# A one-layer adaLN, attention and sparse FFN kernel: the last group's expert marks and spread pattern at full array size

## The chip, the cores and the metric

The kernel runs on one core of one Trainium2 chip. A core has five engines that run side by side and wait for each other through semaphores: TensorE (PE; its matmuls, and apart from them the loads of the stationary operand, PEld), VectorE (DVE), ScalarE (ACT), GpSimd (POOL) and SyncE (SP), which starts most DMAs. The metric is the device time of one execution in microseconds; the kernel before takes 114.97 us, the median of three runs (114.91 to 114.98).

## What is computed

The input is 2048 tokens of 128 features. The reference, cut to what matters:

```python
x = L0_attn_y_all
h = layernorm(x) * (1 + ca) + sa
x = x + ga * attention(h, Wq, bq, Wk, bk, Wv, bv, Wo, bo)       # causal, one head of 128
h = layernorm(x) * (1 + cb) + sb
x = x + gb * ffn(h)

def ffn(x):                                                     # 16 experts, blocks of 32 of 512 channels
    prob = softmax(x @ w_router + b_router)
    _, idx = top_k(prob, 4)
    mask = (idx[:, :, None] == arange(16)).any(axis=1)          # 4 of 16 experts for a token
    h = relu(einsum('nd,ebd->neb', x, w1b) + b1b)
    y = einsum('neb,ebd,ne->nd', h, w2b, mask)
    return y + b2
```

All scale and shift vectors come from `silu(c) @ wmod`. What counts here is the mask: a token's hidden channels of the 12 experts that it did not choose must be zero.

## The kernel before

The tokens are 16 tiles of 128, in 4 groups of 4 tiles (512 tokens). A tile `[P, 512]` holds one group with features or channels on the 128 partitions. Values that need more precision than one pass gives are kept as a high and a low part of type float32r, and a product is three matmuls: high by high, low by high, high by low (`three`, lines 928, 929 and 932). Each engine has its own program, and the order of its steps is written out by hand in a table (`TENSOR_PLAN`, `SCALAR_PLAN`, `VECTOR_PLAN`, `GPSIMD_PLAN`): a letter names a step, a number its tile. Every step begins with the semaphores that it waits for.

On TensorE the last group's end of the plan reads `d8 h11 d9 d10 m3 y0 h12 v12 h13 v13 y1 d11 h14 v14 h15 v15 d12 d13 y2 d14 d15 t0 y3 t1`. Here `h` is an up-projection tile (three matmuls of 512 columns), `d` a down-projection tile (three matmuls), `y` turns a finished group back to rows of tokens (fp32 transposes, line 1168), `t` computes the last two token tiles directly in rows (line 1139), `m` turns the choice of experts and `v` is explained below.

The choice. `choose` on DVE finds a token's four largest router logits and marks them. For groups 0 to 2 it writes each expert's mark eight times over (`chosen`, 128 columns in bf16), `turn_choice` on TensorE transposes four blocks of 128 by 128 into `norm_bank` (line 1108), and ScalarE copies them out as `keep`, by which DVE multiplies the hidden channels (line 841). The four hidden tiles of a group share one `keep`, since the channels are dealt so that partition q of each tile belongs to expert q // 8.

For the last group (`shut_by_tensor`) TensorE does the masking. `choose` writes one mark for each expert, 1 where it was not chosen (`unchosen`, `[P, 4, 16]` bf16, line 826). `turn_choice` transposes them: `unchosen[:, i]` with its 16 columns is the stationary operand and the identity moves, four times (line 1103). ScalarE copies the 16 by 512 result to `shut` (line 637). Then `shut_channels` (`v12` to `v15`, line 1133) adds `spread.T @ shut` to the hidden tile in PSUM; `spread` is 16 by 128 and has -1e30 where a channel belongs to an expert, so each channel of a shut expert falls far below zero and relu makes it zero. ScalarE reads the tile twice (lines 652 and 653, high part and the last 256 columns), and DVE subtracts for the low part (line 850), which the down-projection's third matmul reads.

`spread` is built by GpSimd at the start (`prepare(4)`, lines 502 to 507, fourth step of its plan): memset, two selects that keep a band, one cast. In the plan it stands ahead of `j0`, the first half group's 1/sigma (lines 439 and 440), for which DVE waits before it normalises the first tokens (line 706). A `step` on GpSimd adds to `pool_step` and waits for it; `ahead` adds without waiting.

Of the kernel before, what the change touches and what calls it, by code (L numbers as in the profile page):

```python
# [5 lines left out]
ALU = mybir.AluOpType  # L6
# [4 lines left out]
BF16 = mybir.dt.bfloat16  # L11
# [11 lines left out]
P = 128  # L23
GT = 4
GW = GT * P
EPS = 1e-5
FAR = -1e30
FURTHEST = 3e38
# [42 lines left out]
def adaln_attention_sparse_ffn(nc, x_in, wq_in, bq_in, wk_in, bk_in, wv_in, bv_in, wo_in, bo_in,  # L71
# [3 lines left out]
    NBLK = wr_in.shape[1]  # L75
# [4 lines left out]
    NH = HID // P  # L80
# [52 lines left out]
    with ExitStack() as ctx:  # L133
        def sb(name, shape, dt=F32):
            return ctx.enter_context(nc.sbuf_tensor(name, shape, dt))

        def sem(name):
            return ctx.enter_context(nc.semaphore(name))
# [4 lines left out]
        ctx_bank, norm_bank, proj_bank = bank[5], bank[6], bank[7]  # L143
# [64 lines left out]
        rden = sb("rden", [P, NT])  # L208

        shut_by_tensor = (NG - 1,)  # L210
        shut, spread = sb("shut", [NBLK, GW], BF16), sb("spread", [NBLK, P], BF16)
        spread_full = sb("spread_full", [NBLK, P])
        unchosen = sb("unchosen", [P, GT, NBLK], BF16)


        swung_sums = sb("swung_sums", [P, GT, 2, NBLK])
# [3 lines left out]
        marked = sb("marked", [P, GT, KEYS])  # L220
# [13 lines left out]
        ident_made, copies_made, causal_made, future_made, unseen_made, warm_made, filler_made, base_made, ones_made, keys_made, spread_made = (  # L234
            sem(n) for n in ("ident_made", "copies_made", "causal_made", "future_made", "unseen_made", "warm_made", "filler_made", "base_made", "ones_made", "keys_made", "spread_made"))
# [176 lines left out]
        def _(pool):  # L412
# [6 lines left out]
            def step(ins):  # L419
                ahead(ins)  # L420
                pool.wait_ge(pool_step, steps[0])
# [38 lines left out]
            def prepare(i):  # L460
                if i == 0:
                    pool.memset(pow_half[:], -0.5)
                    step(pool.memset(ident[:], 0.0))
                    pool.affine_select(out=ident[:], in_=ident[:], compare_op=ALU.not_equal, fill=1.0, base=0,
                                       pattern=[[-1, P]], channel_multiplier=1).then_inc(ident_made, 1)
                elif i == 6:
                    pool.wait_ge(mod_out, 1)
                    gates()
                elif i == 1:
                    step(pool.memset(causal_full[:], 0.0))  # L470
                    step(pool.affine_select(out=causal_full[:], in_=causal_full[:], compare_op=ALU.is_ge, fill=FAR, base=0,
                                            pattern=[[-1, P]], channel_multiplier=1))
                    pool.tensor_copy(causal[:], causal_full[:]).then_inc(causal_made, 1)
                elif i == 7:
                    step(pool.memset(future[:, GW - P:], 0.0))
                    pool.affine_select(out=future[:, GW - P:], in_=future[:, GW - P:], compare_op=ALU.is_ge, fill=FAR, base=0,
                                       pattern=[[-1, P]], channel_multiplier=1).then_inc(future_made, 1)
                elif i == 8:
                    step(pool.memset(unseen[:], 0.0))
                    pool.affine_select(out=unseen[:], in_=unseen[:], compare_op=ALU.is_ge, fill=FAR, base=0,  # L480
                                       pattern=[[1, P]], channel_multiplier=-1).then_inc(unseen_made, 1)
                elif i == 9:
                    pool.wait_ge(w1_hi_s, 1)
                    pool.tensor_tensor(w1t_lo[:], w1_full[:], w1t_hi[:].bitcast(F32), ALU.subtract).then_inc(w1_lo_s, 1)
                elif i == 11:
                    pool.wait_ge(wr_full_s, 1)
                    pool.wait_ge(wr_in_s, 32)
                    step(pool.tensor_tensor(wr_full[0:1, :], wr_full[0:1, :], br_row[:], ALU.add))
                    step(pool.tensor_copy(wr_halves[:, 0, :], wr_full[:]))
                    pool.tensor_tensor(wr_halves[:, 1, :], wr_full[:], wr_halves[:, 0, :].bitcast(F32),  # L490
                                       ALU.subtract).then_inc(wr_s, 1)
                elif i == 10:
                    pool.wait_ge(w2_hi_s, 1)
                    pool.tensor_tensor(w2t_lo[:], w2_full[:], w2t_hi[:].bitcast(F32), ALU.subtract).then_inc(w2_lo_s, 1)
                elif i == 12:
                    pool.wait_ge(gbb2_row_s, 1)
                    pool.wait_ge(*emptied(f"o{NG - 1}", 1))
                    for i in range(2):
                        last = pool.tensor_tensor(x_due[:, i, :], x[:, NT - 2 + i, :], gbb2_row[:], ALU.add)
                    last.then_inc(x_due_s, 1)  # L500
                elif i == 4:
                    step(pool.memset(spread_full[:], FAR))
                    step(pool.affine_select(out=spread_full[:], in_=spread_full[:], compare_op=ALU.is_ge, fill=0.0, base=0,
                                            pattern=[[1, P]], channel_multiplier=-PER))
                    step(pool.affine_select(out=spread_full[:], in_=spread_full[:], compare_op=ALU.is_ge, fill=0.0,
                                            base=PER - 1, pattern=[[-1, P]], channel_multiplier=PER))
                    pool.tensor_copy(spread[:], spread_full[:]).then_inc(spread_made, 1)
# [16 lines left out]
        def _(act):  # L524
# [109 lines left out]
            def keep_copy(g):  # L634
                act.wait_ge(chosen_turned, g + 1)
                if g in shut_by_tensor:
                    nc.scalar.copy(shut[:], norm_bank[0:NBLK, 0:GW // 2].bitcast(BF16)).then_inc(keep_s, 1)
                else:
                    keeps, chose = grp(keep, g), norm_bank[:, 0:GW // 2].bitcast(BF16)
                    if g in SWUNG:  # L640
                        keeps = keeps.rearrange("c (i b t) -> c b i t", i=GT, b=GT)
                        chose = chose.rearrange("c (b i t) -> c b i t", i=GT, b=GT)
                    nc.scalar.copy(keeps, chose).then_inc(keep_s, 1)
# [26 lines left out]
        def _(dve):  # L670
# [146 lines left out]
            def choose(g):  # L817
                dve.wait_ge(keys_s, g + 1)
                for i in range(GT):
                    last = nc.vector.max(top8[:, i, :], keys[:, i, :])  # L820
                step(last)
                for i in range(GT):
                    last = nc.vector.match_replace(marked[:, i, :], top8[:, i, :], keys[:, i, :], FURTHEST)
                step(last)
                if g in shut_by_tensor:
                    nc.vector.tensor_scalar(unchosen[:], marked[:, :, 0:NBLK], FURTHEST, None, ALU.is_lt).then_inc(chosen_s, 1)
                    return
                if g >= 1:
                    dve.wait_ge(chosen_turned, g)
                each = marked[:, :, 0:NBLK].rearrange("p i (e o) -> p i e o", o=1).broadcast_to([P, GT, NBLK, PER])  # L830
                nc.vector.tensor_tensor(chosen[:], each, highest(g).rearrange("p (i e o) -> p i e o", e=1, o=1).broadcast_to(
                    [P, GT, NBLK, PER]), ALU.is_gt).then_inc(chosen_s, 1)
# [89 lines left out]
        def _(pe):  # L922
# [176 lines left out]
            def turn_choice(g):  # L1099
                pe.wait_ge(chosen_s, g + 1)  # L1100
                if g in shut_by_tensor:
                    for i in range(GT):
                        last = nc.tensor.transpose(norm_bank[0:NBLK, i * P // 2:(i + 1) * P // 2].bitcast(BF16),
                                                   unchosen[:, i], ident_b[:])
                    last.then_inc(chosen_turned, 1)
                    return
                for i in range(GT):
                    last = nc.tensor.transpose(norm_bank[:, i * P // 2:(i + 1) * P // 2].bitcast(BF16),
                                               chosen[:, i].rearrange("p e k -> p (e k)"), ident_b[:])
                last.then_inc(chosen_turned, 1)  # L1110
# [17 lines left out]

            def shut_channels(n):
                pe.wait_ge(keep_s, n // NH + 1)  # L1130
                if n == NH * shut_by_tensor[0]:
                    pe.wait_ge(spread_made, 1)
                mm(turned_bank(f"h{n}")[:], spread[:], shut[:], start=False, stop=True).then_inc(turn_mm, 1)  # L1133

            def down_rows(i):
# [139 lines left out]
```

## Time and profile before

| what | value |
|---|---|
| time, median of 3 runs | 114.97 us (114.91 to 114.98) |
| span of the profiled execution | 113.2 us, 2012 instructions |
| PE matmuls busy | 109.0 us (96%), x585 |
| PE weight loads busy | 87.6 us (77%) |
| DVE busy | 87.3 us (77%) |
| ACT busy | 74.3 us (66%) |
| POOL busy | 88.1 us (78%) |
| granted TensorE clock, mean | 1.000, that is 2.4 GHz |

The span runs from the first to the last instruction of the one execution that was profiled; its own device time isn't given apart, and the median of the runs stands for it, 1.77 us above the span. The page says that matmuls are pipelined and their ends modelled: two matmuls whose busy times overlap run one behind the other, and the distance of their starts tells what the first cost. A matmul row has a partner on PEld, the load of its stationary operand, which can run under the matmul ahead of it; "idle before" on a PEld row is time in which no load ran. In a row, `128*16` behind the names is rows by columns of the stationary operand, `16*128` likewise.

### The profile page before, as it was taken

Reading aid. Unit: us, or ns where it says so; the run is one execution under the profiler, and the core shown is the slowest. Engines: PE = TensorE matmul, PEld = TensorE weight load, DVE = VectorE, ACT = ScalarE, POOL = GpSimd, SP = SyncE. Lnnn points to the kernel's source line nnn. Section 1 sums busy time; section 2 is a strip of 40 time slices with the busy share of each in tenths; the row PEclk is TensorE's granted clock in tenths of the full one; section 3 lists DMA queues with packets and bytes.
Section 4 is the critical chain, followed back from the end, with each engine's and each line's share of the span. In section 5 each row is a group of like instructions: output and inputs, shape, how many; then the busy total and the mean of one; then the engine's idle time right before and its main releaser. Section 6 shows DMA issues by size and latency. Waiting matters only on the chain.

```text
span 113.2 us, 2012 instructions
## 1 busy us (share of the span) xinstructions
PE 109.0 (96%) x585; PEld 87.6 (77%) x585; DVE 87.3 (77%) x322; ACT 74.3 (66%) x163; POOL 88.1 (78%) x118
## 2 busy tenths in 40 slices
PE   5999999999999999999999999999999999999991
PEld 2588769878888888888877878788898888856590
DVE  5999989999999999978897399708974846854251
ACT  1346398497973499677498995988815578435610
POOL 6869868998999199989899999999992898916000
PEclk9999999999999999999999999999999999999999
DMA  2894000000000000000000000000000000003314
GB/s 60 266 336 130 3 0 6 0 3 0 0 3 0 6 0 0 0 0 3 0 0 6 0 0 0 0 0 0 0 6 3 0 3 0 0 0 93 98 56 129
DMA packets 5879, 3.42 MB, mean 30 GB/s; under 512 B 743, under 2 KB 5483, under 8 KB 5868
## 3 DMA queue, kind: packets, MB, share of 16 engines
q1 hardware_dynamic: 5292, 3.03, 9.0%
q10 hardware_dynamic: 576, 0.26, 0.9%
q8 instruction: 5, 0.08, 0.3%
q14 instruction: 6, 0.05, 0.1%
HBM read 2.24 MB, written 1.05 MB: 29 GB/s over the span
## 4 chain that ended last, share of the span: by engine, by line
PE 81%; DVE 13%; issue 2%; POOL 2%
PE bank L928 14%; PE bank L929 13%; PE bank L932 13%; PE bank L1040 7%; PE bank L988 7%; PE bank L1027 6%; PE bank L1028 6%; PE bank L1072 3%; PE bank L962 2%; PE bank L1168 2%; PE bank L1139 2%; DVE nmax L743 1%; DVE st L686 1%; POOL rstd L440 1%; PE bank L1133 1%
## 5 line engine op out<-in xcount | busy, mean ns | idle before, releaser
L512 POOL TENSOR_TENSOR p_lo<-p_full,p_hi 128x512 fp32r<-128x512 f32 (+2 forms) x36 | 42.5, 1206 | 4.6 <-ACT p_full L626 4.5
L619 ACT ACTIVATE p_hi<-bank 128x512 fp32r<-128x512 f32 (+2 forms) x36 | 20.6, 571 | 6.6 <-PE bank L932 2.9
L626 ACT ACTIVATE p_full<-bank 128x512 f32<-128x512 f32 (+2 forms) x36 | 20.5, 568 | 0.6 <-POOL p_lo L512 0.6
L518 POOL TENSOR_TENSOR hid_lo<-hid_full,hid_hi 128x512 fp32r<-128x512 f32 x12 | 15.4, 1294 | 5.3 <-ACT hid_hi L655 5.3
L748 DVE TENSOR_REDUCE cmax<-bank 128x1 f32<-128x512 f32 x24 | 16.1, 685 | 2.0 <-PE bank L988 1.7
L1027 PE MATMUL bank<-g_hi,zt_hi 128*128 128x512 f32 (+3 forms) x40 | 15.2, 381 | 0.0
L1040 PE MATMUL bank<-g_lo,zt_hi 128*128 128x512 f32 (+3 forms) x40 | 14.6, 373 | 0.2 <-DVE g_lo L768 0.2
L1028 PE MATMUL bank<-g_hi,zt_lo 128*128 128x512 f32 (+3 forms) x40 | 14.6, 364 | 0.0
L928 PE MATMUL bank<-p_hi,z_hi 128*128 128x512 f32 (+2 forms) x36 | 14.0, 389 | 0.0
L988 PE MATMUL bank<-zt_hi,g_hi 128*128 128x512 f32 (+3 forms) x40 | 13.8, 386 | 0.0
L929 PE MATMUL bank<-p_hi,z_lo 128*128 128x512 f32 (+2 forms) x36 | 13.5, 374 | 0.0
L932 PE MATMUL bank<-p_lo,z_hi 128*128 128x512 f32 (+2 forms) x36 | 13.4, 373 | 0.0
L841 DVE SCALAR_TENSOR_TENSOR hid_full<-bank,keep 128x512 f32<-128x512 f32 x12 | 8.1, 686 | 5.6 <-POOL hid_lo L518 2.7
L590 ACT ACTIVATE xn<-x,mean_rstd,rstd 128x127 f32<-128x127 f32 x24 | 9.9, 485 | 0.3 <-POOL mean_rstd L433 0.3
L655 ACT CAST hid_hi<-hid_full 128x512 fp32r<-128x512 f32 x12 | 7.4, 622 | 3.0 <-DVE hid_full L841 2.4
L1040 PEld LDWEIGHTS bank<-g_lo,zt_hi 128*128 128x128 f32 x40 | 7.5, 188 | 1.8 <-issue 0.7
L988 PEld LDWEIGHTS bank<-zt_hi,g_hi 128*128 128x128 f32 x40 | 7.5, 189 | 1.4 <-ACT g_hi L605 0.2
L1027 PEld LDWEIGHTS bank<-g_hi,zt_hi 128*128 128x128 f32 x40 | 7.5, 189 | 1.1
L1028 PEld LDWEIGHTS bank<-g_hi,zt_lo 128*128 128x128 f32 x40 | 7.6, 189 | 0.9
L430 POOL TENSOR_TENSOR rstd<-rstd,pow_half 128x4 f32<-128x4 f32 x7 | 7.3, 1038 | 0.6
L928 PEld LDWEIGHTS bank<-p_hi,z_hi 128*128 128x128 f32 x36 | 6.8, 188 | 1.2
L932 PEld LDWEIGHTS bank<-p_lo,z_hi 128*128 128x128 f32 x36 | 6.8, 188 | 1.2
(212 smaller groups left out, 256.1 us busy)
## 6 DMA issues: line engine op xcount, KB each, us to landing
x<-in_L_attn_y_all_dram SPq DMA_DIRECT2D x3, 256.0 KB, 3.5
out_dram<-res SPq DMA_DIRECT2D x3, 256.0 KB, 2.3
w<-in_L_ffn_w_dram SPq DMA_DIRECT2D x2, 256.0 KB, 4.2
x<-in_L_attn_y_all_dram SPq DMA_DIRECT2D x2, 128.0 KB, 2.9
wmod<-in_L_wmod_dram SPq DMA_DIRECT2D x1, 256.0 KB, 3.7
wmod<-in_L_wmod_dram ACTq DMA_DIRECT2D x1, 128.0 KB, 3.2
out_dram<-res SPq DMA_DIRECT2D x1, 128.0 KB, 1.9
wk<-in_L_attn_Wk_dram SPq DMA_DIRECT2D x1, 64.0 KB, 2.9
```

The source lines that it names most:

```text
L512: pool.tensor_tensor(p_lo[:, s, w:], p_full[:, n % 2, w:], p_hi[:, s, w:].bitcast(F32), ALU.subtract).then_inc(p_lo_pool, 1)
L518: pool.tensor_tensor(hid_lo[:, m, :], hid_full[:, n % 2, :], hid_hi[:, m, :].bitcast(F32), ALU.subtract).then_inc(hid_lo_pool, 1)
L619: nc.scalar.activation(p_hi[:, s, w:], src, ACT.Exp).then_inc(p_hi_s, 1)
L626: nc.scalar.activation(p_full[:, n % 2, w:], src, ACT.Exp).then_inc(p_full_s, 1)
L748: nc.vector.tensor_reduce(cmax[:, n, c:c + 1], src, AX.X, ALU.max, negate=True).then_inc(turn_out, 1)
L928: mm(dst, w_hi, m_hi, start=start, stop=False)
L929: mm(dst, w_lo, m_hi, start=False, stop=False)
L932: return mm(dst, w_hi, m_lo, start=False, stop=stop)
L988: last = mm(dst[:, 0:w], tile(g_hi, g * GT + r), zt_hi[:, c * GW:c * GW + w], start=True, stop=not masked)
L1027: mm(dst[:, w:], tile(zt_hi, j), high, start=True, stop=False)
L1028: mm(dst[:, w:], tile(zt_lo, j), high, start=False, stop=False)
L1040: last = mm(dst[:, w:], tile(zt_hi, j), g_lo[:, g * GW + w:(g + 1) * GW], start=False, stop=not diag)
```

## The change

Three tensors of the last group's choice get the full array size. `unchosen` has 128 columns for each token tile, of which GpSimd clears the last 112 at the start; `spread` and `spread_full` have 128 rows, in which the selects leave rows 16 to 127 at zero; `shut` has 128 rows, which the transposes fill with the turned marks and zeros. DVE still writes 16 marks for each token tile. The wait for `spread_made` stands ahead of the transposes instead of ahead of the first shut matmul. The plans are unchanged.

```diff
@@ -208,9 +208,9 @@
         rden = sb("rden", [P, NT])
 
         shut_by_tensor = (NG - 1,)
-        shut, spread = sb("shut", [NBLK, GW], BF16), sb("spread", [NBLK, P], BF16)
-        spread_full = sb("spread_full", [NBLK, P])
-        unchosen = sb("unchosen", [P, GT, NBLK], BF16)
+        shut, spread = sb("shut", [P, GW], BF16), sb("spread", [P, P], BF16)
+        spread_full = sb("spread_full", [P, P])
+        unchosen = sb("unchosen", [P, GT, P], BF16)
 
 
         swung_sums = sb("swung_sums", [P, GT, 2, NBLK])
@@ -499,6 +499,7 @@
                         last = pool.tensor_tensor(x_due[:, i, :], x[:, NT - 2 + i, :], gbb2_row[:], ALU.add)
                     last.then_inc(x_due_s, 1)
                 elif i == 4:
+                    ahead(pool.memset(unchosen[:, :, NBLK:], 0.0))
                     step(pool.memset(spread_full[:], FAR))
                     step(pool.affine_select(out=spread_full[:], in_=spread_full[:], compare_op=ALU.is_ge, fill=0.0, base=0,
                                             pattern=[[1, P]], channel_multiplier=-PER))
@@ -634,7 +635,7 @@
             def keep_copy(g):
                 act.wait_ge(chosen_turned, g + 1)
                 if g in shut_by_tensor:
-                    nc.scalar.copy(shut[:], norm_bank[0:NBLK, 0:GW // 2].bitcast(BF16)).then_inc(keep_s, 1)
+                    nc.scalar.copy(shut[:], norm_bank[:, 0:GW // 2].bitcast(BF16)).then_inc(keep_s, 1)
                 else:
                     keeps, chose = grp(keep, g), norm_bank[:, 0:GW // 2].bitcast(BF16)
                     if g in SWUNG:
@@ -823,7 +824,7 @@
                     last = nc.vector.match_replace(marked[:, i, :], top8[:, i, :], keys[:, i, :], FURTHEST)
                 step(last)
                 if g in shut_by_tensor:
-                    nc.vector.tensor_scalar(unchosen[:], marked[:, :, 0:NBLK], FURTHEST, None, ALU.is_lt).then_inc(chosen_s, 1)
+                    nc.vector.tensor_scalar(unchosen[:, :, 0:NBLK], marked[:, :, 0:NBLK], FURTHEST, None, ALU.is_lt).then_inc(chosen_s, 1)
                     return
                 if g >= 1:
                     dve.wait_ge(chosen_turned, g)
@@ -1099,8 +1100,9 @@
             def turn_choice(g):
                 pe.wait_ge(chosen_s, g + 1)
                 if g in shut_by_tensor:
+                    pe.wait_ge(spread_made, 1)
                     for i in range(GT):
-                        last = nc.tensor.transpose(norm_bank[0:NBLK, i * P // 2:(i + 1) * P // 2].bitcast(BF16),
+                        last = nc.tensor.transpose(norm_bank[:, i * P // 2:(i + 1) * P // 2].bitcast(BF16),
                                                    unchosen[:, i], ident_b[:])
                     last.then_inc(chosen_turned, 1)
                     return
@@ -1128,8 +1130,6 @@
 
             def shut_channels(n):
                 pe.wait_ge(keep_s, n // NH + 1)
-                if n == NH * shut_by_tensor[0]:
-                    pe.wait_ge(spread_made, 1)
                 mm(turned_bank(f"h{n}")[:], spread[:], shut[:], start=False, stop=True).then_inc(turn_mm, 1)
 
             def down_rows(i):
```

TensorE, from the last group's `m3` on, before (`bank` is PSUM; `128x128` or `16x128` is the output):

```order
L1103 MATMUL bank<-ident_b,unchosen 16x128 [waits chosen_s]
L1103 MATMUL bank<-ident_b,unchosen 16x128 x3
L1168 MATMUL bank<-ident,y_sb 128x128 [waits y_out,ctx_out]
L1168 MATMUL bank<-ident,y_sb 128x128 x3
L928 MATMUL bank<-h_hi,w1t_hi 128x512 [waits nt_lo_s,turn_out]
L929 MATMUL bank<-h_hi,w1t_lo 128x512
L932 MATMUL bank<-h_lo,w1t_hi 128x512
L1133 MATMUL bank<-shut,spread 128x512 [waits spread_made,keep_s]
```

The same place in the changed kernel:

```order
L1105 MATMUL bank<-ident_b,unchosen 128x128 [waits spread_made,chosen_s]
L1105 MATMUL bank<-ident_b,unchosen 128x128 x3
L1168 MATMUL bank<-ident,y_sb 128x128 [waits y_out,ctx_out]
L1168 MATMUL bank<-ident,y_sb 128x128 x3
L929 MATMUL bank<-h_hi,w1t_hi 128x512 [waits nt_lo_s,turn_out]
L930 MATMUL bank<-h_hi,w1t_lo 128x512
L933 MATMUL bank<-h_lo,w1t_hi 128x512
L1133 MATMUL bank<-shut,spread 128x512 [waits keep_s]
```

The four transposes have an output of 128 rows, and the wait for `spread_made` has moved from the first shut matmul to them. The order of the matmuls is the same; line numbers move by one or two.

GpSimd at the start, between the causal pattern and the first 1/sigma:

```order
 L471 AFFINE_SELECT causal_full<-causal_full 128x128
 L473 CAST causal<-causal_full 128x128
-L502 MEMSET spread_full 16x128
-L503 AFFINE_SELECT spread_full<-spread_full 16x128
-L505 AFFINE_SELECT spread_full<-spread_full 16x128
-L507 CAST spread<-spread_full 16x128
+L502 MEMSET unchosen 128x4x112
+L503 MEMSET spread_full 128x128
+L504 AFFINE_SELECT spread_full<-spread_full 128x128
+L506 AFFINE_SELECT spread_full<-spread_full 128x128
+L508 CAST spread<-spread_full 128x128
```

One memset of 4 by 112 elements on each partition stands ahead of the four steps of `spread`, which have 128 partitions; lines 439 and 440, the first 1/sigma, come behind them as before.

## Rows read from the trace of the kernel before

**Rows 1.** The page's chain that ended last: shares by engine and line.

```profile
PE 81%; DVE 13%; issue 2%; POOL 2%
PE bank L928 14%; PE bank L929 13%; PE bank L932 13%; PE bank L1040 7%; PE bank L988 7%; PE bank L1027 6%; PE bank L1028 6%; PE bank L1072 3%; PE bank L962 2%; PE bank L1168 2%; PE bank L1139 2%; DVE nmax L743 1%; DVE st L686 1%; POOL rstd L440 1%; PE bank L1133 1%
```

**Rows 2.** Timeline, last group, TensorE: start us, us, engine, what [idle].

```profile
99.68 0.40 PE L932 MATMUL bank<-hid_lo,w2t_hi 128*128 128x512 f32 x1
100.01 0.39 PE L1103 MATMUL bank<-ident_b,unchosen 128*16 128x128 bf16 x4
...
100.74 0.48 PE L928 MATMUL bank<-h_hi,w1t_hi 128*128 128x512 f32 x1
...
101.29 0.39 PE L932 MATMUL bank<-h_lo,w1t_hi 128*128 128x512 f32 x1
101.60 0.09 PEld L1133 LDWEIGHTS bank<-shut,spread 16*128 16x128 bf16 x1 [0.36 <-issue]
...
102.25 0.39 PE L929 MATMUL bank<-h_hi,w1t_lo 128*128 128x512 f32 x1
...
102.49 0.40 PE L932 MATMUL bank<-h_lo,w1t_hi 128*128 128x512 f32 x1
...
103.54 0.48 PE L928 MATMUL bank<-hid_hi,w2t_hi 128*128 128x512 f32 x1
...
106.00 0.40 PE L932 MATMUL bank<-h_lo,w1t_hi 128*128 128x512 f32 x1
...
106.88 0.28 PE L929 MATMUL bank<-hid_hi,w2t_lo 128*128 128x256 f32 x1
```

**Rows 3.** Timeline of TensorE around group 1's choice, bf16 between fp32r.

```profile
73.47 0.39 PE L932 MATMUL bank<-p_lo,z_hi 128*128 128x512 f32 x1
73.70 0.40 PE L1108 MATMUL bank<-ident_b,chosen 128*128 128x128 bf16 x4
73.91 0.48 PE L928 MATMUL bank<-p_hi,z_hi 128*128 128x512 f32 x1
74.23 0.39 PE L929 MATMUL bank<-p_hi,z_lo 128*128 128x512 f32 x1
```

**Rows 4.** Timeline of TensorE at group 0's router, 32-column stationary operand.

```profile
56.51 0.39 PE L1083 MATMUL bank<-h_hi,wr_halves 128*32 128x512 f32 x1
...
56.97 0.28 PE L928 MATMUL bank<-p_hi,z_hi 128*128 128x256 f32 x1
```

**Rows 5.** TensorE's timeline: four fp32 transposes and the next matmul.

```profile
94.39 0.60 PE L962 MATMUL bank<-ident,xn 128*128 128x128 f32 x4
...
94.75 0.48 PE L928 MATMUL bank<-hid_hi,w2t_hi 128*128 128x512 f32 x1
```

**Rows 6.** Timeline: who feeds TensorE in the last group, and one reader.

```profile
99.25 0.19 DVE L826 TENSOR_SCALAR unchosen<-marked 128x64 bf16<-128x64 f32 x1
...
100.43 0.57 ACT L637 COPY shut<-bank 16x512 bf16<-16x512 bf16 x1 [2.54 <-PE bank L1103]
...
107.51 0.43 DVE L850 SCALAR_TENSOR_TENSOR hid_lo<-bank,hid_hi 128x256 fp32r<-128x256 f32 x1 [0.78 <-ACT hid_last L653]
...
108.50 0.28 PE L932 MATMUL bank<-hid_lo,w2t_hi 128*128 128x256 f32 x1
```

**Rows 7.** GpSimd's memsets by line: count | busy us, mean ns | idle.

```profile
L470 POOL MEMSET causal_full<- 128x128 f32 x1 | 0.2, 210 | 0.0
...
L462 POOL MEMSET pow_half<- 128x4 f32 x1 | 0.1, 102 | 0.3 <-POOLq L1262 0.3
```

**Rows 8.** Timeline of the start, GpSimd and one memset of DVE.

```profile
2.59 0.91 DVE L913 MEMSET nmax<- 128x1024 f32 x1 [0.16 <-issue]
...
2.73 0.99 POOL L503 TENSOR_SCALAR_AFFINE_SELECT spread_full<-spread_full 16x128 f32<-16x128 f32 x1
...
3.79 0.28 POOL L505 TENSOR_SCALAR_AFFINE_SELECT spread_full<-spread_full 16x128 f32<-16x128 f32 x1
...
4.67 0.25 POOL L439 TENSOR_SCALAR rstd<-mv 128x2 f32<-128x2 f32 x1 [0.25 <-DVE mv L698]
```

## Prediction

> **What bounds the kernel now.** I read the page's chain of waits first. It ends last on TensorE: 81% of the span is PE, 13% DVE, 2% POOL [rows 1]. So what a change takes from PE comes off the end, if nobody whom PE waits for is late. The change touches PE in one stretch, the last group's choice and hidden layer, so I opened the timeline of PE and its weight loads from 99.6 to 108.6 us, and looked at it by start times. The page models when a matmul ends, so a column "busy" shows PE without a gap there; the distance from one start to the next shows what a matmul costs.
>
> Between full-array matmuls the distance is steady: 0.23 us for 512 columns (73.47 to 73.70) [rows 3]. Around the last group's narrow operations it isn't. The up-projection's third matmul starts at 101.29, the weights of the shut matmul with its 16 rows load only at 101.60, 0.31 behind it and after 0.36 us in which the load path did nothing. The second matmul of the next tile starts at 102.25, so from 101.29 to there it takes 0.96 us [rows 2]. The reader is to see a pause ahead of the narrow matmul, and another behind it.
>
> Is it the pause or the type? The nearest control in the same kernel is the choice of the other groups: four bf16 transposes, 128 by 128, between fp32r matmuls. They start 0.23 after the matmul ahead (73.70), the next fp32r matmul 0.21 after them (73.91), and only there are 0.08 to 0.09 lost, since its weights had no long matmul to hide behind (73.91 to 74.23 is 0.32) [rows 3]. A change of type alone has no pause ahead of it, and 512 bf16 columns take 0.21.
>
> **The change part by part.**
>
> Choice of the last group (line 1103 to 1105). It removes 16-column stationary operands, and puts 128-column ones there; four transposes stay four. From 99.68 to the start of the next tile at 100.74 it is 1.06 us now, with 0.33 of it up to the first transpose at 100.01 [rows 2]. With full operands it is 0.23 up to them and 0.21 for them [rows 3], and 0.36 for the four fp32 transposes of y behind them (94.39 to 94.75) [rows 5]: 0.80, or 0.88 with the 0.08 of the uncovered weight load. Saving 0.18 to 0.26; I take 0.20.
>
> The four shut matmuls (line 1133), the wide part of the sum. Now 16 rows, then 128. The first: 0.96 us now; 0.23 + 0.21 + 0.24 = 0.68 with full operands, where the 512 columns cover the next weight load: 0.28. The second has the y transposes behind it: 102.49 to 103.54 is 1.05 now, 0.23 + 0.21 + 0.36 = 0.80 then: 0.25. The third has the same neighbours as the first: 0.28. The fourth has 256-column matmuls behind it, for which I take half of 0.23: 106.00 to 106.88 is 0.88 now, 0.23 + 0.21 + 0.12 = 0.56 then: 0.32 [rows 2, 3, 5]. Together 1.13, with the choice 1.33 us. Bounds: 0 if the pauses stay, 1.39 with the choice at 0.26.
>
> A narrow output alone need not pay. The router's fp32r matmuls have a 32-column stationary operand, and two of them and their exit take 0.46 (56.51 to 56.97), twice 0.23 [rows 4]. So the 0.20 at the choice is the less certain part: there the operand is narrow in columns, at the shut matmuls in rows. The Trainium skill, TensorEngine Tiling (Array Packing), section Key Properties, says that changing the tiling mode drains TensorE. Taken for every operand narrower than the array it would have the router pay as well, and the trace disagrees there; for bf16 operands of 16 rows or columns the trace agrees, with the 0.31 and 0.33 above. By the rule the sum is 1.33, and if columns never paid it would be 1.13.
>
> Who is late once PE is faster? The first shut matmul wants `shut`: ScalarE copies it from 100.43 for 0.57 us, to 101.00, for a matmul that starts at 101.60 [rows 2, 6]. PE arrives there 0.28 earlier (0.20 at the choice and 0.08 ahead of the shut matmul), at about 101.32, and the copy ends about 0.1 earlier: 0.4 us of slack. That copy now covers 128 partitions instead of 16 with the same 512 elements each; I cost it at nothing, since the count of elements on a partition is what it was. The tightest place is the end: DVE's last remainder ends at 107.51 + 0.43 = 107.94, and the matmul that reads it starts at 108.50, 0.56 later [rows 6]. Of what PE gains, 0.24 lies between the shut matmul that feeds this remainder and its reader (0.32 less the 0.08 ahead of it), so 0.32 is left. Everything else there moves up with PE.
>
> DVE's mark at line 826 writes its 64 elements in four pieces 128 apart instead of in one. It ends at 99.25 + 0.19 = 99.44 [rows 6], and PE wants it at 99.68 + 0.23 = 99.91: 0.4 us cover it, so nothing. The wait on `spread_made` goes one PE step earlier; GpSimd is past making it by 4.67 [rows 8], and it is needed at 99.9: nothing, and nothing queues behind it.
>
> GpSimd's clearing of the padding (line 502), the one cost. It stands in front of four steps that are followed by the first 1/sigma (line 439), and line 440 stands in the chain of what ended last [rows 1]. 448 bf16 elements per partition: a memset of 4 took 0.10, of 128 took 0.21, so about 0.87 ns an element and 0.49 us if each counts one, 0.29 if two go together [rows 7]. GpSimd sat idle for 0.25 before line 439, waiting for DVE [rows 8]. So the delay is 0.49 - 0.25 = 0.24 by the one price, and 0.04 by the other. Another thing can hide it: the first select of `spread_full` took 0.99 us where the second took 0.28; it ran beside DVE's 0.91 us memset (2.59 to 3.50) [rows 8]. If it was held until about then, a memset ahead of it only eats held time. Bounds 0 and 0.24; that `spread_full` has 128 partitions instead of 16 in three steps is inside them. I take 0.10, between the held time and the price of the two-byte elements. That delay passes through whole: line 440, DVE's line 686 and the maxima of line 743 all stand in the chain [rows 1].
>
> The Trainium skill, SBUF — State Buffer, section Who interferes with whom, says that a DVE instruction with at most one SBUF input outside its two-port modes doesn't contend with GpSimd. No run here shows whether it holds for this memset. By the rule the 0.7 us aren't DVE's, nothing is eaten, and the cost is up to 0.24.
>
> Sum: -1.33 + 0.10 = -1.23 us. The profiled span is 113.2 us, the median of the three runs 114.97; the 1.77 us around the span don't change. 114.97 - 1.23 = 113.74, and the span about 111.95.
>
> **Rivals.**
>
> *The pauses are not the narrow operand's.* Then the shape changes and nothing is gained, and GpSimd's cost stays. For it: the router's rows, narrow and without a pause. Against: those are fp32r, and every bf16 operand with 128 by 128 is clean. 114.97 + 0.00 to 0.10, so 115.0 to 115.07. Chance 0.06.
>
> *Half of it.* Only the pause ahead or only that behind goes, or rows pay and columns don't and a waiting engine takes some. The pauses ahead are 0.10 at the choice and 0.08 at each shut matmul, 0.42; those behind are the other 0.91. 114.97 - 0.42 + 0.10 = 114.65; 114.97 - 0.91 + 0.10 = 114.15. For it: the choice's narrow side is another one than the shut matmuls'. Chance 0.14.
>
> *The start loses more than the end gains (slower).* The padding's clearing is two-byte and in four pieces; if it runs at twice the price per element it takes 0.10 + 0.77 = 0.87, so 0.87 - 0.25 = 0.62 on the chain from the first 1/sigma. It decides once PE gains under 0.62 - 0.23 = 0.39, that is in the first rival's world: 114.97 + 0.62 = 115.6. With PE's gain it would still be 114.25. For it: none of my rows shows a two-byte memset on GpSimd. Against: it needs the pauses to stay as well. Chance 0.05.
>
> **How the numbers follow.** The forecast has 0.75, with its own range from 113.5 (choice at 0.26, start at nothing, and 0.08 for a schedule that falls better) to 114.05 (choice at nothing, start at 0.24). The half case reaches to 114.65; I take it up to 114.3: 113.5 to 114.3. A measurement of this kernel tells apart about 0.2%, 0.23 us. Faster: 0.75 + 0.14, less a little for the unknown, 0.88. Within 0.2%: 0.06. Slower: 0.06.
>
> **What would show it.** In the timeline after: each shut matmul 0.23 to 0.24 behind the one ahead, its weights loading without 0.36 of idle time, the next start 0.21 behind it, and the second matmul of the next tile at 0.24 and not 0.33. The choice's first transpose 0.23 behind. Third, the step to the first 1/sigma at 4.67 or up to 0.24 later, and all DVE starts with it. Wrong if the starts around line 1133 stay 0.31 apart or more; wrong in the other way if they close up but PE then waits for `shut`, for hid_lo, or for y. Equal spacing with an unchanged end would mean that the stretch was not what ended last.

## The result and the profile after

The changed kernel takes 113.72 us, the median of four runs (113.55 to 113.94), against 114.97 for the kernel before; the ratio is 0.9889, with a 95% interval of 0.9871 to 0.9906 (it counts a fourth run of the kernel before, of 115.23). Measured again in another session, it was 0.9884 (0.9858 to 0.9909). The forecast was 113.74.

The profiled execution took 113.55 us, with a span of 111.8 us: 1.4 us less than before. First the page after: busy times and instructions by engine, and the chain that ended last by engine.

```profile
PE 107.3 (96%) x585; PEld 87.3 (78%) x585; DVE 87.3 (78%) x322; ACT 74.4 (67%) x163; POOL 88.1 (79%) x119
...
PE 81%; DVE 13%; issue 2%; POOL 2%
```

PE ends last with the same share as before [rows 1]. PE's busy time fell from 109.0 to 107.3, by 1.7, which is more than the 1.4 us of the span: it counts modelled ends and is no measure of what was saved. The starts are. The timeline of TensorE and of one weight load in the last group, columns as in [rows 2]:

```profile
99.59 0.40 PE L933 MATMUL bank<-hid_lo,w2t_hi 128*128 128x512 f32 x1
...
99.83 0.40 PE L1105 MATMUL bank<-ident_b,unchosen 128*128 128x128 bf16 x4
...
100.43 0.48 PE L929 MATMUL bank<-h_hi,w1t_hi 128*128 128x512 f32 x1
...
100.98 0.39 PE L933 MATMUL bank<-h_lo,w1t_hi 128*128 128x512 f32 x1
101.20 0.10 PEld L1133 LDWEIGHTS bank<-shut,spread 128*128 128x128 bf16 x1 [0.27 <-issue]
101.21 0.39 PE L1133 MATMUL bank<-shut,spread 128*128 128x512 bf16 x1
...
101.67 0.40 PE L930 MATMUL bank<-h_hi,w1t_lo 128*128 128x512 f32 x1
...
101.91 0.40 PE L933 MATMUL bank<-h_lo,w1t_hi 128*128 128x512 f32 x1
...
102.73 0.47 PE L929 MATMUL bank<-hid_hi,w2t_hi 128*128 128x512 f32 x1
...
103.97 0.40 PE L933 MATMUL bank<-h_lo,w1t_hi 128*128 128x512 f32 x1
...
104.67 0.40 PE L930 MATMUL bank<-h_hi,w1t_lo 128*128 128x512 f32 x1
...
104.91 0.40 PE L933 MATMUL bank<-h_lo,w1t_hi 128*128 128x512 f32 x1
...
105.50 0.28 PE L930 MATMUL bank<-hid_hi,w2t_lo 128*128 128x256 f32 x1
```

The reader is to see the first transpose 0.24 behind the matmul ahead (99.59 to 99.83; 0.33 before), and the first shut matmul 0.23 behind its own (100.98 to 101.21; 0.31 to its weights before). Behind it the second matmul of the next tile starts at 101.67. The third place, before, stands in the same view of the kernel before:

```profile
104.79 0.40 PE L932 MATMUL bank<-h_lo,w1t_hi 128*128 128x512 f32 x1
...
105.77 0.39 PE L929 MATMUL bank<-h_hi,w1t_lo 128*128 128x512 f32 x1
```

Read in the same way as the prediction did, from the matmul ahead to the one that a pause can no longer reach:

| place | before, us | predicted | after | gain |
|---|---|---|---|---|
| choice, then y | 1.06 | 0.80 to 0.88 | 0.84 | 0.22 |
| 1st shut matmul | 0.96 | 0.68 | 0.69 | 0.27 |
| 2nd, then y | 1.05 | 0.80 | 0.82 | 0.23 |
| 3rd | 0.98 | 0.28 less, as the 1st | 0.70 | 0.28 |
| 4th, then 256 columns | 0.88 | 0.56 | 0.59 | 0.29 |
| sum | 4.93 | | 3.64 | 1.29 |

Then who feeds PE, the tightest reader and the last instruction that computes, against [rows 6]:

```profile
100.27 0.59 ACT L638 COPY shut<-bank 128x512 bf16<-128x512 bf16 x1 [2.47 <-PE bank L1105]
...
106.34 0.42 DVE L851 SCALAR_TENSOR_TENSOR hid_lo<-bank,hid_hi 128x256 fp32r<-128x256 f32 x1 [0.51 <-ACT hid_last L654]
...
107.13 0.28 PE L933 MATMUL bank<-hid_lo,w2t_hi 128*128 128x256 f32 x1
...
109.45 0.29 DVE L902 TENSOR_TENSOR res<-bank,x_due 128x128 f32<-128x128 f32 x1 [0.20 <-PE bank L1139]
```

`shut` is copied by 100.27 + 0.59 = 100.86, 0.35 ahead of the matmul that wants it at 101.21; the copy of 128 partitions takes 0.59, that of 16 took 0.57. DVE's last remainder ends at 106.34 + 0.42 = 106.76, and its reader starts at 107.13: 0.37 are left of 0.56. Nobody became late. DVE's last sum starts at 109.45, against 110.82 before.

The start of GpSimd and the first 1/sigma, against [rows 8]:

```profile
2.46 0.47 POOL L502 MEMSET unchosen<- 128x448 bf16 x1
...
3.14 0.58 POOL L504 TENSOR_SCALAR_AFFINE_SELECT spread_full<-spread_full 128x128 f32<-128x128 f32 x1
...
4.67 0.25 POOL L439 TENSOR_SCALAR rstd<-mv 128x2 f32<-128x2 f32 x1 [0.22 <-DVE mv L699]
```

The added memset took 0.47 us, and still line 439 starts at 4.67, as before. The select behind it took 0.58 instead of 0.99 and ended at 3.72, as before (2.73 + 0.99, 3.14 + 0.58). So the start cost nothing.

The profile is 0.09 ahead already where the stretch begins (99.59 against 99.68). I don't put it down to the change: the kernels of the experiments below, which have the same work up to there, reach this point anywhere from 99.54 to 100.16 in their profiles (64 and 96 columns). Most of the late one can be traced: in the profiled execution with 96 columns TensorE waited for the transfer (DMA) of the FFN weights `w`, and the transposes of `w` (line 1218 there) started at 8.65, where the kernel before has them at 8.14. The second profile of the changed kernel shows the same wait (8.70, in an execution of 114.20). Such a late transfer makes one execution about 0.5 us longer, and it has nothing to do with the change.

### The profile page after: what moved, and what is told of

Its sections match the earlier page's. It is cut to its first block, busy times and chain, and to the rows that moved or that the text cites. A ratio compares the mean times of both kernels' runs of the same rounds, so it can differ in the third digit from the quotient of the medians.

```text
span 111.8 us, 2013 instructions
## 1 busy us (share of the span) xinstructions
PE 107.3 (96%) x585; PEld 87.3 (78%) x585; DVE 87.3 (78%) x322; ACT 74.4 (67%) x163; POOL 88.1 (79%) x119
## 3 DMA queue, kind: packets, MB, share of 16 engines
HBM read 2.24 MB, written 1.05 MB: 29 GB/s over the span
## 4 chain that ended last, share of the span: by engine, by line
PE 81%; DVE 13%; issue 2%; POOL 2%
PE bank L929 14%; PE bank L930 13%; PE bank L933 13%; PE bank L1041 8%; PE bank L989 7%; PE bank L1029 6%; PE bank L1028 6%; PE bank L1073 3%; PE bank L963 2%; PE bank L1139 2%; DVE nmax L744 1%; DVE st L687 1%; PE bank L1168 1%; POOL rstd L440 1%; DVE xn L714 1%
```

## The experiments

The theory: TensorE pauses ahead of and behind a bf16 operation whose stationary operand is narrower than the array, in rows or in columns; the five places are worth about 1.3 us and nothing else in the change matters. The rivals: columns don't pay, the pause is a matter of type, each narrow matmul pays for itself, the moved wait did it, the start lost or won something. Of each edit only the lines that carry it are printed; the slices that go with a width change with it. Unless said otherwise the times stand beside 114.95 and 114.92 us, the medians of the kernel before in those two sessions.

**Only rows.** The choice is transposed from 16 columns as before; `shut` and `spread` have 128 rows, and GpSimd clears `shut` instead of the padding.

```diff
-        unchosen = sb("unchosen", [P, GT, P], BF16)
+        unchosen = sb("unchosen", [P, GT, NBLK], BF16)
-                    ahead(pool.memset(unchosen[:, :, NBLK:], 0.0))
+                    ahead(pool.memset(shut[:], 0.0))
-                    nc.scalar.copy(shut[:], norm_bank[:, 0:GW // 2].bitcast(BF16)).then_inc(keep_s, 1)
+                    nc.scalar.copy(shut[0:NBLK, :], norm_bank[0:NBLK, 0:GW // 2].bitcast(BF16)).then_inc(keep_s, 1)
```

> Only the shut matmuls' operands have 128 rows (rows 16 to 127 cleared at the start by one GpSimd memset of 512 bf16 elements); the choice is transposed from 16 columns as before. Theory (a bf16 stationary operand narrower than the array pauses TensorE ahead of it and behind it, in rows and in columns alike): the four shut places fall from 0.96, 1.05, 0.98, 0.88 to 0.69, 0.82, 0.70, 0.59 us, the choice stays at 1.06; about 1.07 faster than before, 113.9. Rival (only the columns of the transposes pay, and the shut matmuls gain as a consequence of the full transposes): the shut places stay, 114.97. Rival (the whole gain lies in the order of waits): 113.7 or 114.97.

It took 113.92 us, ratio 0.9911 (0.9896 to 0.9926). The timeline of TensorE, the choice and the first shut matmul:

```profile
99.65 0.40 PE L933 MATMUL bank<-hid_lo,w2t_hi 128*128 128x512 f32 x1
...
100.71 0.48 PE L929 MATMUL bank<-h_hi,w1t_hi 128*128 128x512 f32 x1
...
101.27 0.39 PE L933 MATMUL bank<-h_lo,w1t_hi 128*128 128x512 f32 x1
...
101.96 0.40 PE L930 MATMUL bank<-h_hi,w1t_lo 128*128 128x512 f32 x1
```

The choice still takes 1.06 (99.65 to 100.71); the four others take 0.69, 0.82, 0.71 and 0.57 (the first is shown, 101.27 to 101.96). The gain in starts is 1.08, that in time 1.03.

**Only columns.** The reverse: the choice has 128 columns, the shut matmuls read 16 rows.

```diff
-                mm(turned_bank(f"h{n}")[:], spread[:], shut[:], start=False, stop=True).then_inc(turn_mm, 1)
+                mm(turned_bank(f"h{n}")[:], spread[0:NBLK, :], shut[0:NBLK, :], start=False, stop=True).then_inc(turn_mm, 1)
```

> Only the choice's transposes get 128 columns; the shut matmuls read the first 16 rows of the same tensors. Theory: the choice falls from 1.06 to 0.84 us, the shut places stay at 0.96, 1.05, 0.98, 0.88; 0.2 faster than before, 114.75. Rival (columns never pay, as the router's 32 columns don't): 114.97, choice at 1.06.

It took 114.66 us, ratio 0.9979 (0.996 to 0.9997).

```profile
99.63 0.40 PE L933 MATMUL bank<-hid_lo,w2t_hi 128*128 128x512 f32 x1
...
100.47 0.48 PE L929 MATMUL bank<-h_hi,w1t_hi 128*128 128x512 f32 x1
...
101.02 0.39 PE L933 MATMUL bank<-h_lo,w1t_hi 128*128 128x512 f32 x1
...
101.99 0.39 PE L930 MATMUL bank<-h_hi,w1t_lo 128*128 128x512 f32 x1
```

Now the choice takes 0.84, 0.22 less, and the first shut matmul 0.97, as before; over all five places the starts gain 0.20. Two parts, each with its own gain: 0.20 and 1.08, within 0.01 the 1.29 of the whole. In time it is 0.29, with an interval of 0.03 to 0.46. The doubt of the prediction, that columns might not pay, is gone for these bf16 transposes: it had put 0.20 on them.

**64 and 96.** All three tensors with 64, and with 96, instead of 128.

```diff
-        shut, spread = sb("shut", [P, GW], BF16), sb("spread", [P, P], BF16)
-        unchosen = sb("unchosen", [P, GT, P], BF16)
+        WIDE = 64
+        shut, spread = sb("shut", [WIDE, GW], BF16), sb("spread", [WIDE, P], BF16)
+        unchosen = sb("unchosen", [P, GT, WIDE], BF16)
```

> All three tensors get 64 rows and columns instead of 128. Theory with a step (anything that leaves part of the array unused switches it, whatever the width): all five places stay as before, 114.9 to 115.0. Rival (the pause shrinks with the unused part): about half the gain, 114.35. Rival (only the smallest quarter of the array pays): the whole gain, 113.7.

> All three tensors get 96 rows and columns. Theory with a step: 96 is either a partly used full array, and then the five places are as in the change (0.84, 0.69, 0.82, 0.70, 0.59), 113.7; or it is narrow like 16, and then 114.97. Rival (the pause shrinks with the unused part): three quarters of the gain, 114.05.

64 took 114.9 us, ratio 0.9998 (0.9983 to 1.0013), and 96 took 113.64, ratio 0.9898 (0.9879 to 0.9917). The first shut matmul with 64 rows:

```profile
101.17 0.39 PE L934 MATMUL bank<-h_lo,w1t_hi 128*128 128x512 f32 x1
101.50 0.39 PE L1134 MATMUL bank<-shut,spread 64*128 64x512 bf16 x1
...
102.16 0.39 PE L931 MATMUL bank<-h_hi,w1t_lo 128*128 128x512 f32 x1
```

And with 96 rows:

```profile
101.52 0.39 PE L934 MATMUL bank<-h_lo,w1t_hi 128*128 128x512 f32 x1
101.75 0.39 PE L1134 MATMUL bank<-shut,spread 96*128 96x512 bf16 x1
...
102.21 0.40 PE L931 MATMUL bank<-h_hi,w1t_lo 128*128 128x512 f32 x1
```

With 64 all five places are as before (1.08, 0.99, 1.05, 0.99, 0.87), with 96 as in the change (0.81, 0.69, 0.82, 0.70, 0.59). It is a step, not a slope, and it lies between 64 and 96: 96 is as good as 128, and 64 is worth nothing. The run with 64 also settles a rival: it has the moved wait for `spread_made` and a memset of the padding like the changed kernel, and gains nothing, so neither of them is the cause. The Trainium skill, TensorEngine Tiling (Array Packing), section Tiling Modes, lists tiles of 128, 64 and 32 rows or columns, and its section Key Properties says that a change of mode drains the engine. By that rule 64 is a mode of its own, while 96 isn't in the list and would take the whole array; these two runs agree. The router's float32r operand doesn't: 32 columns are in the list, and it has no pause [rows 4].

**Pairs of narrow matmuls.** The kernel before, with the shut matmuls side by side.

```diff
-    d10 m3 y0 h12 v12 h13 v13 y1 d11 h14 v14 h15 v15 d12 d13 y2 d14 d15 t0 y3 t1
+    d10 m3 y0 h12 h13 v12 v13 y1 d11 h14 h15 v14 v15 d12 d13 y2 d14 d15 t0 y3 t1
```

> The kernel before with 16 rows, but the shut matmuls stand in pairs: h12 h13 v12 v13 and h14 h15 v14 v15 instead of h12 v12 h13 v13 and so on. Theory (the pause belongs to the change between narrow and full, not to each narrow matmul): v13 follows v12, and v15 follows v14, after 0.21 to 0.31 with no pause ahead, two of the eight pauses pairs go, 0.5 us of TensorE; v14 and v15 come later for ScalarE and VectorE, so 0.1 may be given back: 114.5 to 114.6. Rival (each narrow matmul pays for itself): v12 to v13 0.4 or more, 114.97 or above.

It took 114.37 us, ratio 0.9952 (0.9935 to 0.9969): 0.55 faster; 114.5 to 114.6 was expected.

```profile
102.02 0.40 PE L932 MATMUL bank<-h_lo,w1t_hi 128*128 128x512 f32 x1
102.35 0.60 PE L1133 MATMUL bank<-shut,spread 16*128 16x512 bf16 x2
102.88 0.66 PE L1168 MATMUL bank<-ident,y_sb 128*128 128x128 f32 x4
```

0.33 ahead of the pair, and 0.53 from its first start to the transposes; one alone took 0.32 to there before (102.81 to 103.13), so the second narrow matmul costs 0.21, its 512 columns. The pause belongs to the change between narrow and full, and two narrow ones in a row share it.

**16 rows of float32r.** The kernel before, with `shut` and `spread` as float32r.

```diff
-        shut, spread = sb("shut", [NBLK, GW], BF16), sb("spread", [NBLK, P], BF16)
+        shut, spread = sb("shut", [NBLK, GW], F32R), sb("spread", [NBLK, P], F32R)
```

> The kernel before with spread and shut as float32r instead of bf16, still 16 rows; the choice stays 16 columns of bf16. Theory (few rows pause TensorE whatever the type): the four shut places stay at 0.9 to 1.05 us or grow by up to 0.1 each, as float32r weights load for 0.11 to 0.19 us and not 0.09; 115.0 to 115.3. Rival (only bf16 operands pay, since the router's float32r operand of 32 columns is clean): the four places fall to 0.70, 0.81, 0.70, 0.58; 113.9.

It took 115.31 us, ratio 1.003 (1.0018 to 1.0042): slower.

```profile
101.35 0.39 PE L932 MATMUL bank<-h_lo,w1t_hi 128*128 128x512 f32 x1
101.67 0.50 PE L1133 MATMUL bank<-shut,spread 16*128 16x512 f32 x1
102.10 0.50 PE L928 MATMUL bank<-h_hi,w1t_hi 128*128 128x512 f32 x1
102.43 0.39 PE L929 MATMUL bank<-h_hi,w1t_lo 128*128 128x512 f32 x1
```

The pause ahead stays at 0.32, and the matmul with its weights takes 0.43 where bf16 took 0.31. The place is 1.08 instead of 0.96, and 0.09 to 0.12 longer each time. So 16 rows pause TensorE in either type. The longer weight load is a likely reason for the rest (its row in the trace takes 0.18 us where bf16's takes 0.09), but no run takes it apart. The router's 32 columns of float32r remain without a pause [rows 4]: in that type these 32 columns don't pay, 16 rows do.

**The start: two more memsets.** The changed kernel, with 0.82 us more of GpSimd's work ahead of the first 1/sigma.

```diff
                     ahead(pool.memset(unchosen[:, :, NBLK:], 0.0))
+                    for k in range(2):
+                        ahead(pool.memset(spare[:, k], 0.0))
```

> The changed kernel with two more GpSimd memsets of the same size (448 bf16 elements, into a spare tensor) right behind the first, ahead of the first 1/sigma. Theory (the changed kernel's memset cost nothing, because GpSimd's first select is held until 3.7 us and there were 0.25 us of idle time): 0.82 more work, of which 0.30 comes out at line 439, which starts at about 4.97 instead of 4.67, and all of it at the end: 114.0. Rival (the select's extra time is its own): line 439 at 5.27, 114.3. Rival (the start has slack elsewhere): 113.72.

It took 114.03 us, ratio 0.9947 (0.9911 to 0.9984). Seven of its ten runs took 113.98 to 114.10, the other three 115.11 to 115.46, so the interval is wide, and the reading rests on the trace. The timeline of the start:

```profile
2.86 0.88 POOL L505 MEMSET spare<- 128x448 bf16 x2
...
3.42 0.55 DVE L919 COPY base<-ident 128x128 f32<-128x128 f32 x1
...
3.96 0.29 POOL L507 TENSOR_SCALAR_AFFINE_SELECT spread_full<-spread_full 128x128 f32<-128x128 f32 x1
...
5.10 0.25 POOL L440 TENSOR_SCALAR rstd<-mv 128x2 f32<-128x2 f32 x1
```

The select that had taken 0.58 took 0.29 once it began at 3.96. But GpSimd wasn't what came out late. The third memset still ran when VectorE's copy of the identity began; the copy took 0.55 instead of 0.16, all of VectorE's later work moved by 0.42, and the 1/sigma waited for it: 5.10 instead of the expected 4.97. The last sum starts at 109.88 instead of 109.45, so the 0.43 went through whole in the trace. The time came out as expected (114.0), but not by the path expected: GpSimd's work was to come out late by 0.30, and it was VectorE's copy that did.

**The start: the long memset of VectorE elsewhere.** The changed kernel, with `nmax` cleared behind the three copies.

```diff
-            nc.vector.memset(nmax[:], 0.0).then_inc(ones_made, 1)
             dve.wait_ge(ident_made, 1)
             step(nc.vector.tensor_copy(base[:], ident[:]))
             nc.vector.memset(base[0:1, 1:], -1.0).then_inc(base_made, 1)
             nc.vector.tensor_copy(ident_b[:], ident[:]).then_inc(copies_made, 1)
+            nc.vector.memset(nmax[:], 0.0).then_inc(ones_made, 1)
```

> The changed kernel with VectorE's memset of nmax (0.91 us, 2.59 to 3.50) moved behind its three copies of the identity, so that it runs at about 3.0 to 3.9. Theory (that memset holds GpSimd's select): the select ends later, at about 4.1 and not at 3.72, or is held for the new time of the memset; the first 1/sigma comes up to 0.3 later: 113.75 to 114.1. Rival (the hold is something else at a fixed time): the select still ends at 3.72, and the time is 113.7 to 113.85, since only VectorE's first statistics move by 0.1.

It took 113.58 us, ratio 0.9882 (0.9868 to 0.9897).

```profile
2.22 0.43 POOL L473 CAST causal<-causal_full 128x128 bf16<-128x128 f32 x1
2.35 0.16 DVE L915 COPY base<-ident 128x128 f32<-128x128 f32 x1
...
2.60 0.47 POOL L502 MEMSET unchosen<- 128x448 bf16 x1
...
2.68 0.46 DVE L917 CAST ident_b<-ident 128x128 bf16<-128x128 f32 x1
...
2.99 0.91 DVE L918 MEMSET nmax<- 128x1024 f32 x1
...
3.35 0.29 POOL L504 TENSOR_SCALAR_AFFINE_SELECT spread_full<-spread_full 128x128 f32<-128x128 f32 x1
```

The select runs at 3.35 beside that memset (2.99 to 3.90) and takes 0.29. So the memset isn't what holds it, and neither of the two expectations was met: the select isn't held at all, so nothing at a fixed time holds it either. The cast of the identity, which now runs beside GpSimd's memset, is held instead (0.46, not 0.15). And the hold has moved with VectorE's copy of the identity: the copy now begins at 2.35, and GpSimd's cast of the causal pattern, begun ahead of it at 2.22, takes 0.43 instead of 0.29. The Trainium skill, SBUF — State Buffer, section Who interferes with whom, says that a VectorE instruction with at most one SBUF input outside the two-port modes doesn't contend with GpSimd, and that copies and casts can enter a two-port mode, in which the one that issues first gets the shared ports for the whole instruction and the other blocks. The trace agrees for the memset (0.29 beside it) and for the cast of the identity (0.46). It disagrees on who blocks for the causal cast, which began first and was the one held. What was left for the select was the copy that stands right behind the long memset.

**The start: one column between.** The kernel before, with a memset of one column between the long memset and the copy.

```diff
             nc.vector.memset(nmax[:], 0.0).then_inc(ones_made, 1)
+            nc.vector.memset(warm2[:], 0.0)
             dve.wait_ge(ident_made, 1)
             step(nc.vector.tensor_copy(base[:], ident[:]))
```

> The kernel before with one VectorE memset of a single column (0.06 us) between the memset of nmax and the copy of the identity; nothing else. Theory (GpSimd's first select is held by the identity's copy that stands next in VectorE's queue behind the long memset, from the moment it is next): the copy is no longer next until 3.5 us, so the select that starts at 2.73 takes 0.29 and not 0.99. Rival (it is held by something at a fixed time, or its time is its own): still about 0.99. The total stays at 114.9 to 115.05 either way, as GpSimd waits for VectorE there afterwards.

It took 115.01 us beside 115.1 for the kernel before in that session, ratio 0.9989 (0.9974 to 1.0005).

```profile
2.72 0.28 POOL L504 TENSOR_SCALAR_AFFINE_SELECT spread_full<-spread_full 16x128 f32<-16x128 f32 x1
...
3.42 0.28 POOL L508 CAST spread<-spread_full 16x128 bf16<-16x128 f32 x1
3.43 0.35 DVE L917 COPY base<-ident 128x128 f32<-128x128 f32 x1
...
4.87 0.25 POOL L440 TENSOR_SCALAR rstd<-mv 128x2 f32<-128x2 f32 x1 [1.17 <-DVE mv L699]
```

The select takes 0.28 instead of 0.99, beside the same 0.91 us memset of VectorE. The copy as it stood in the kernel before:

```profile
3.42 0.16 DVE L915 COPY base<-ident 128x128 f32<-128x128 f32 x1
```

There the select, begun at 2.73, ended at 3.72, 0.14 behind the end of this copy (3.58). The causal cast of the run before ended 0.14 behind its copy as well (2.65 and 2.51). So the reading that fits every run is that the select was held by the copy that stood next in VectorE's queue, from about 0.7 us before that copy itself began; how a waiting copy does that, no run shows. The theory of this run holds, but GpSimd, early now, is in the cast when the copy comes, and the copy is held in turn: 0.35 instead of 0.16. VectorE's chain starts 0.20 later (4.87 against 4.67). One of the two pays in both kernels; in the kernel before the one that paid had idle time. In the trace these 0.20 reach the end: the last sum starts at 111.03 instead of 110.82, which the expectation had ruled out. The times don't show them (the interval ends 0.06 above the kernel before, whose 17 runs in that session scatter from 114.86 to 115.76), and that difference stays open.

**Once more, side by side.** The changed kernel as it is, and with the later memset, in one session beside the same 115.1.

> The changed kernel as it is, beside the next one on the same chip: 113.7, 1.2 under before.

> The changed kernel with VectorE's memset of nmax behind its copies of the identity, once more beside the changed kernel. If the 0.05 us by which the first 1/sigma came earlier reaches the end: 0.05 to 0.1 under the changed kernel, 113.6. Rival: no difference that can be told.

113.89 us, ratio 0.9884 (0.9858 to 0.9909), and 113.70 us, ratio 0.9876 (0.985 to 0.9903). The first 1/sigma is 0.05 earlier in the second one's trace; whether the time is, these runs can't tell.

## Why the prediction was right, point by point

- **The bound.** Right. PE ended last before and after; 1.29 us less in the starts of five places is 1.4 of span with the 0.09 from ahead of them, and 1.25 of time (1.1 to 1.5 by the interval).
- **The four shut matmuls**, 1.13 predicted, 1.07 measured in the starts (0.27, 0.23, 0.28, 0.29). The pieces taken from the other groups' choice and from the plain f32r distances held; each place is 0.01 to 0.03 longer than they add up to.
- **The choice**, 0.20 predicted, 0.22 measured, and shown apart by the run with columns only. The doubt about columns was rightly left open: the router's rows are evidence for float32r alone.
- **The signs in the timeline.** Most were met (0.23 to the shut matmul and to the choice's first transpose, 4.67 for the first 1/sigma), two were not. The shut matmul's weights still load after 0.27 us of idle time, and the next start is shown 0.04 behind the shut matmul and the second matmul of the tile 0.42 behind that, instead of 0.21 and 0.24. Only the sum, 0.46 against 0.45, is as forecast. The load of group 1's full choice in the kernel before has 0.26 us of idle time too, though its matmul starts 0.23 behind the one ahead [rows 3], so the idle time was no sign to go by.
- **The type.** The prediction argued from [rows 3] that bf16 between float32r doesn't pause. The run with 16 rows of float32r shows the other side: without the change of type the pause stays (0.32 ahead).
- **Who is late.** Nobody: 0.4 predicted for `shut`, 0.35 found; 0.32 predicted for the last remainder, 0.37 found.
- **The start**, 0.10 predicted, 0.00 measured: the term that was off. The price of the memset was right (0.49 predicted, 0.47 found), and so was the guess that held time would swallow it. What held the select was named wrong: not VectorE's memset beside it but the copy queued behind. The sum of -1.23 came within 0.02 of the measured -1.25 because this 0.10 stands against the 0.04 that the five places gave less, and the time shows 0.04 less again than the starts. That closeness is luck: the interval of the measured time is 0.2 us to either side. Three of its sums are off by a little, without weight for the forecast: the upper end of its own range is 114.08 and not 114.05 (114.97 - 1.13 + 0.24), and the rivals' 114.15 and 114.25 are 114.16 and 114.26.
- **The rivals.** "Half of it": in the whole change both pauses went at every place, and columns and rows each gave their own part, 0.20 and 1.08. "The pauses are not the narrow operand's" fell with the same two runs and with 64 against 96. For the start that loses more than the end gains, the price per element of the two-byte memset was the normal one; with 0.82 us more it loses 0.43 in the trace up to the last sum, which shows that such a start does reach the end.

## What to carry to other kernels

If a small bf16 matmul or transpose stands alone between full ones, compare the distances of the starts with those of a full one, not the busy times: here each cost 0.22 to 0.29 us more than its columns, and padding it with zeros to more than 64 rows or columns (96 did, 64 didn't) took that away, at a memset of 0.47 us somewhere idle. Rows were tried here with matmuls and columns with transposes only, and a float32r operand of 32 columns paid nothing. If it can't be padded, put narrow ones side by side, so that they share the pauses. And before a cheap setup step is put on GpSimd or VectorE, see which copies of the other engine stand next in the queue there: at the start of this kernel 0.4 us of such a collision reached the end whole in the trace.

## What was not expected of the hardware

- A full bf16 weight load is shown at the start of its own matmul, with 0.27 us of idle time ahead, and not under the matmul ahead like the float32r ones; yet the starts show no cost (0.23 to the shut matmul and 0.46 from it to the second matmul of the next tile, which is two distances of full matmuls). The next float32r load is shown in the same moment. The idle time on a PEld row alone doesn't prove a pause.
- 96 of 128 rows or columns behave like all of them, 64 like 16.
- GpSimd's select was held for 0.7 us by a VectorE copy that hadn't begun, but only stood next (that the two share ports is the account of the Trainium skill, SBUF — State Buffer, Who interferes with whom; the runs show only who was held when, and here the one that began first was held); GpSimd's memsets in the same time weren't (0.47 and 0.20 us, their usual prices). One more instruction of 0.06 us between freed it. A memset isn't free of it altogether: with the later memset of VectorE, GpSimd's memset of `spread_full` began at 3.01 while VectorE's cast still ran (2.68 to 3.14), and took 0.28 instead of 0.20.
